# A hybrid layer stack over eight sequences: the loop over the sequences written out as straight code

## The reference

```python
def _layernorm(x): return (x - mean(x)) / sqrt(var(x) + 1e-5)

x = x + retention(_layernorm(x))      # 4 heads, chunks of tokens with a decaying state, gate, out projection
x = x + channel_mix(_layernorm(x))    # token shift, sigmoid(xr @ W_r) * (relu(xk @ W_k)**2 @ W_v)
x = x + attention(_layernorm(x))      # 16 heads of 16 features, softmax(q k / 4 + relative bias) v, out projection
x = x + channel_mix(_layernorm(x))    # the same weights as before
```

## Time and profile before

| | |
|---|---|
| median of three runs | 3388.71 us |
| lowest, highest | 3387.69, 3392.32 us |
| span of the profiled execution, first to last instruction | 3385.0 us |
| the profiled execution's own time | not given beside its span; the median is 3.7 us above the span |
| instructions recorded | 51303 |
| busy: PE, PEld | 3038.8 us (90%), 1389.2 us (41%) |
| busy: DVE, ACT, POOL | 2054.3 us (61%), 1713.4 us (51%), 1304.5 us (39%) |
| DMA | 108.66 MB, mean 32 GB/s |

### The profile page before, as it was taken

The page is one execution under the profiler, slowest core; times in us unless marked ns, Lnnn a source line. Parts: engine busy times, 40 slices in busy tenths (PEclk is TensorE's granted clock), DMA queues, the critical chain, the costliest instruction groups (busy, mean ns, idle before and its releaser), DMA issues.

```text
span 3385.0 us, 51303 instructions
## 1 busy us (share of the span) xinstructions
PE 3038.8 (90%) x14692; PEld 1389.2 (41%) x14692; DVE 2054.3 (61%) x3333; ACT 1713.4 (51%) x3668; POOL 1304.5 (39%) x1816
## 2 busy tenths in 40 slices
PE   6979999799997999879998799988999789997898
PEld 4623266223661236512365133652346523464224
DVE  4568645686456854478544785447854478544784
ACT  2427733377343763337633476334763347533575
POOL 2324533244332443424434244342443334433344
PEclk8979999799997999979999799997999979998899
DMA  5050000500004000140001300023000320003200
GB/s 147 13 112 1 2 14 13 112 2 1 14 24 101 1 1 14 42 83 1 1 14 51 75 1 1 14 58 68 2 7 8 68 58 1 8 8 74 51 1 13
DMA packets 71931, 108.66 MB, mean 32 GB/s; under 512 B 10896, under 2 KB 33472, under 8 KB 71488
## 3 DMA queue, kind: packets, MB, share of 16 engines
q1 hardware_dynamic: 71616, 104.91, 13.3%
HBM read 70.07 MB, written 36.72 MB: 32 GB/s over the span
## 4 chain that ended last, share of the span: by engine, by line
PE 64%; issue 8%; DVE 8%; DMA 7%; ACT 5%; POOL 4%; SPq 2%; ACTq 0%; DVEq 0%; POOLq 0%
PE psum L629 13%; PE psum L607 13%; PE psum L578 12%; PE psum L478 10%; PE psum L682 3%; DVE mx L1248 3%; DMA SQ<-mrow 2%; DMA SK<-parts 2%; ACT Z L999 2%; PE psum L663 2%; PE psum L723 2%; PE psum L497 2%; DMA parts<-Z 2%; POOL X L1338 2%; PE psum L709 2%
## 5 line engine op out<-in xcount | busy, mean ns | idle before, releaser
L1248 DVE TENSOR_REDUCE mx<-psum 128x1 f32<-128x1024 f32 x1024 | 1205.1, 1219 | 411.0 <-PE psum L578 411.0
L999 ACT ACTIVATE Z<-psum 128x512 f32<-128x512 f32 x2048 | 1103.5, 598 | 482.0 <-PE psum L607 479.7
L1426 POOL TENSOR_TENSOR Z<-Z,band_exp 128x256 f32<-128x256 f32 (+1 forms) x1152 | 713.0, 640 | 1040.2 <-ACT Z L999 1029.4
L578 PE MATMUL psum<-SK,SQ 96*128 96x512 bf16 x2048 | 626.2, 426 | 117.6 <-DMA SK<-parts 94.1
L607 PE MATMUL psum<-SQ,SK 128*128 128x512 bf16 x2048 | 647.7, 389 | 93.5 <-DMA SQ<-mrow 67.6
L629 PE MATMUL psum<-Z,Vx 128*17 128x512 f32 x4096 | 538.3, 599 | 4.2
L607 PEld LDWEIGHTS psum<-SQ,SK 128*128 128x128 bf16 x2048 | 165.4, 97 | 725.5 <-ACT Z L999 581.3
L478 PE MATMUL psum<-Wqkvg,Z 128*128 128x512 f32 x768 | 374.5, 614 | 25.0 <-ACT Z L906 22.5
L578 PEld LDWEIGHTS psum<-SK,SQ 96*128 96x128 bf16 x2048 | 189.7, 101 | 476.1 <-DVE mx L1248 179.3
L1368 POOL TENSOR_TENSOR Z<-Z 128x512 f32<-128x512 f32 x64 | 81.2, 1269 | 313.2 <-DVE Z L1177 313.2
L478 PEld LDWEIGHTS psum<-Wqkvg,Z 128*128 128x128 f32 x768 | 137.4, 191 | 153.5 <-issue 150.5
(11 more groups left out here) (124 smaller groups left out, 3363.6 us busy)
## 6 DMA issues: line engine op xcount, KB each, us to landing
parts<-Z SPq DMA_DIRECT2D x96, 256.0 KB
Xin<-L_attn_a_x SPq DMA_DIRECT2D x9, 1024.0 KB, 5.6
out<-X SPq DMA_DIRECT2D x16, 512.0 KB, 3.2
SQ<-parts SPq DMA_DIRECT2D x16, 384.0 KB, 6.4
SQ<-parts SPq DMA_DIRECT2D x24, 256.0 KB, 9.1
SK<-parts SPq DMA_DIRECT2D x16, 384.0 KB, 8.2
SK<-parts SPq DMA_DIRECT2D x24, 256.0 KB, 11.8
SQ<-parts SPq DMA_DIRECT2D x8, 768.0 KB, 8.8
```

The costliest lines, as they stand in the source:

```text
L578: mm = pe.matmul(bank[2 * (u % 2) + k], SQ[0:MAX_ROW, h, i * P:i * P + P], SK[0:MAX_ROW, h, 512 * k:512 * k + 512], start=True, stop=True)
L999: nc.scalar.activation(ring[:, n % RING, :], col_bank(s, c), ACT.Exp)\
L1248: nc.vector.tensor_reduce(mx[:, blk, col:col + 1], bank_pair[u % 2], AX_X, ALU.max)\
L1426: nc.gpsimd.tensor_tensor(ring[:, n % RING, a:z], ring[:, n % RING, a:z], band_exp[:, 4 * hg + c, at:at + z - a], ALU.mult)\
```

## The change

The five `Fori` loops become Python loops. `b` is then a number when the stream is written: the body stands eight times in each engine's stream, the loop's register, addition and branch are gone, and every value that a wait compares with is a constant. Work, order, tiles, semaphores and DMAs stay the same. The addresses of the loads of x and of the stores of the output, which depend on b, become constants too.

```diff
-            with sp.Fori(0, B) as b:
+            for b in range(B):
...
-            with pe.Fori(0, B) as b:
+            for b in range(B):
...
-            with act.Fori(0, B) as b:
+            for b in range(B):
...
-            with dve.Fori(0, B) as b:
+            for b in range(B):
...
-            with pool.Fori(0, B) as b:
+            for b in range(B):
```

## The result

The straight code is slower. Median of five runs 3399.81 us (3394.32 to 3403.2) against 3388.71 us of the kernel before; ratio 1.0027, 95% interval 1.0014 to 1.0039. The prediction was 3372.6 us and faster, its range 3361 to 3384: wrong in sign. The profiled execution took 3394.32 us, its span is 3392.3 us, 7.3 us more than the 3385.0 before.

What follows compares the result with a forecast made beforehand. TensorE held 64% of the chain, "issue" 8%; each sequence's end began with DVE's jump stall. Span 3385.0 - 13.6 (jumps) - 1.0 (register arithmetic) - 1.5 (clock) = 3368.9; with the median 3.7 over the span, 3372.6 us, range 3361 to 3384.

Steps and rivals of the forecast that it cites:

- The seven jumps: At seven sequence ends, straight code removes DVE's stall at the jump back and the whole gain arrives: minus 13.6 us.
- its 0.52 us: PE's idle time left before L478 at a sequence's end, the rest of its jump being hidden behind queued L527 matmuls.
- The register arithmetic: In all engines' streams, waits on registers become waits on constants, nearly all beside running instructions: minus 1.0 us.
- plus 1.2 us: Worst end of the register term: PE's double wait ahead of L478 costs 19 ns more on each of 64 token tiles.
- W: Follow-up theory, not in the prediction: attention's first exponential has its late wait on a separate instruction, 60 ns more, 27 us.
- the bodies were to keep their length to 0.5: Sign expected in the profile after: bodies between the sequence ends keep their length to 0.5 us.
- The clock: Short clock falls, as at the fifth sequence's start, become less likely with a shorter wait: minus 1.5 us, ends minus 5, plus 4.
- A: Rival, 9%: at the sequence ends L1171 waits for another result, only about 0.5 us returns at each of seven: 3385.1 us.
- B: Rival, 4%: at the sequence ends the jump is cheap, the 1.9 us have another cause; 2.1 us back at most: 3386.6.
- D: Rival, 5%: straight code arrives late through the instruction queues, about 3.5 us per late packet; ten late packets give 3408 us.
- a new "issue" of 2 us inside a sequence: Sign that the prediction is wrong: new idle time by "issue" of 2 us or more inside a sequence, pointing to D.
- C: Rival, 8%: register arithmetic in the engines' streams matters, its 10 us bound is used up: 3363.6 us.

## Why the prediction was wrong

**The seven jumps: right, mechanism and size.** Forecast 13.6 us, measured 13.3. L1029 follows L1308 directly, DVE's "issue" wait there is gone, and L1171 stands 0.24 us behind L1308, where under 0.4 was asked. L748 waits 1.20 us where 0.85 was forecast, mostly since PE came earlier: its last L473 ends 463.63 - 460.19 = 3.44 us behind L1308, where 3.70 was worked out; L748 itself starts 4.63 behind it, where 4.55 was. DVE's jump alone is worth 11.1 us in the part with the ends (367.4 to 356.3), PE's alone nothing (368.0), as the prediction had it: its 0.52 us count only once DVE's is gone.

**The register arithmetic: the step that failed.** The prediction wrote that an ALU_OP "that carries the first of two waits must, I assume, be replaced by an EVENT_SEMAPHORE that does", and counted 18 ns less on ACT. So it took the first of two waits to stay on the separate instruction. It did not: the first wait is now the instruction's own, and the second, at the exponential the late one, went to the EVENT_SEMAPHORE. The second error was to price the separate instruction by its own 17 or 51 ns, and not by the time from the semaphore's rise to the start of the work. That is 23 ns without one in the way and 83 with, and the row of durations can't show it. The third was to bound the cost by the share of the sequencers in the chain; this bounds what taking register instructions away can gain, not what a wait moved behind one can cost. The end of "plus 1.2 us" took a double wait of PE ahead of L478 for 19 ns dearer; it became 71 ns cheaper (113 to 42). Measured: +28.2 us in the attention, against 60 ns x 457 = 27 us by W. So the term that was put at minus 1.0 us, with plus 1.2 as its worst, has +28.2 us in the attention against it, and very likely the 12.8 us less in retention and first mix for it (see below). Per sequence that is 3.5 us more and 1.6 less, where the bodies were to keep their length to 0.5.

**Why 60 ns count in full.** In the chain of before, L999 has 2% and L607 and L629 26%, so I took the attention for PE's.

```profile
PE psum L629 13%; PE psum L607 13%; PE psum L578 12%; PE psum L478 10%; PE psum L682 3%; DVE mx L1248 3%; DMA SQ<-mrow 2%; DMA SK<-parts 2%; ACT Z L999 2%; PE psum L663 2%; PE psum L723 2%; PE psum L497 2%; DMA parts<-Z 2%; POOL X L1338 2%;
```

But PE and ACT are tied there: PE's fourth score matmul waits for the second exponential, which follows the first, which waits for the first matmul; and behind the fourth matmul PE has the weighing and then the next step's first matmul, in its own order. The list of waits said so, had I read it for this stage: ACT waited for L607 821 times, and PE's weight load of L607 for ACT 968 times. Each waits for the other in nearly every step, and that is a cycle, whatever engine the chain names.

**What the same term gained elsewhere.** Retention and first mix became 12.8 us shorter. The single engines give 4.1 (DVE), 1.7 (ACT) and 5.2 (PE), 11.0 in sum, but each is hardly more than what two profiles of one kernel differ by; the 12.8 us as a whole are not: the seven profiles with DVE, PE and POOL straight have 1199 to 1204 us there, the two with no straight code 1213.7 and 1216.5. The idle time of PE's weight loads of L478 fell from 153.5 to 143.6 us, before and after:

```profile
L478 PEld LDWEIGHTS psum<-Wqkvg,Z 128*128 128x128 f32 x768 | 137.4, 191 | 153.5 <-issue 150.5
```

```profile
L478 PEld LDWEIGHTS psum<-Wqkvg,Z 128*128 128x128 f32 x768 | 137.3, 190 | 143.6 <-issue 110.0 <-ACT Z L906 30.4
```

Most of what "issue" lost, 30.4 us, is the wait for z_T under its right name: it stood on an ALU_OP before and is L478's own now. The same turn, here for the better, is in the trace at other places of the retention, where the late wait is the one written first. From the semaphore's rise to the start it was 97 ns at ACT's L920, 102 at L927 and 113 at DVE's L1197, and is now 22 to 25. What each of them is worth was not tried by itself.

**The clock.** The kernel before had three short falls of 3.4 us each, at 1712.5 us, 2132.3 and 2927.7; after there is none. In the stretch of the first, from 8.6 us ahead of the fifth sequence's first L748, the granted clock is now 1.00:

```profile
1710.30:1730.30 20.00, 18.07 (x70) 10.34 (x69) 9.66 (x22) 7.00 (x22) 6.87 (x8) 1.00 0.08 27
```

The mean over the span went from 0.938 to 0.942. The direction is as forecast, the size of 1.5 us can't be told from the rest.

**The rivals.** A (something else takes the gain) and B (cheap jumps) fell: L748 waits 1.1 us less at the first end, and 13.3 us came back at the seven. D fell as a mechanism, though its sign came true: there are fewer instruction packets, and turning two waits round took the whole loss away. Its sign of being wrong, a new "issue" of 2 us inside a sequence, can mislead here: the view after has eight of up to 2.5 us ahead of PE's loads of L488, but the same waits stood there before, up to 2.6 us each, under DVE's L1131. The prediction, for its part, found no such "issue" before but at the jumps, and passed over one of 10.8 us on PE's loads of L607; it is a wait for a DMA and stands under that name after, with 10.9. The Trainium skill, "Runtime: NRT & Kernel Launch", section Instruction fetch mechanics, says that a taken branch to a target outside the two pages held needs a DMA fetch first; the trace agrees, as far as the 1.9 us of DVE's idle time vanish with the branch and the instruction packets become fewer. It adds that this is one reason why kernels prefer full unrolling; here that alone made the time 0.27% longer. C (the register arithmetic matters, 3363.6 us) had the gain nearly right, hidden by the turned wait: with the late wait first at seven places the time is 3366.5 and 3364.6 us. So the forecast's 3372.6 needed ACT's loop left as it was, and C's time the waits in the right order. No rival was the case that came: a second effect of the same edit, on the order of two waits, larger than the jumps and of the other sign.

## What to carry to other kernels

When waits change their form, from a register's value to a constant or back, look in the compiled program or the trace which wait of each pair the instruction itself carries, and see to it that it is the one that ends last. Here, with constants, that is the wait written first, with registers the one written last; turned the wrong way it costs 60 to 80 ns on ACT each time that the engine stands waiting. And before costing such an edit at nothing, look for pairs of engines that wait for each other in every step: in the cycle here ACT's 60 ns counted in full, though the chain names PE.

## What was not expected of the hardware

- From a semaphore's rise to the start of the instruction that waits for it, medians by the trace's semaphore events. ACT: 23 ns if the instruction carries the wait, 77 to 83 with an EVENT_SEMAPHORE ahead that carries it, 97 to 102 with an ALU_OP. DVE: 24, 92 to 101, 112 to 117. PE's weight load: 42, 105, 113. POOL: 68 if it carries the wait, and with an EVENT_SEMAPHORE ahead 133 (L1368, L1426), 155 (L1382) or, where that one holds two waits, 176 (L1322). The recorded durations of these instructions (17 to 51 ns) tell less than that.
- An ALU_OP that waits for nothing adds nothing to it on POOL: 68 ns ahead of L1368 and L1426.
- Straight code eight times as long brought fewer instruction packets: 118 and 92 on the two queues, where the loops had 143 and 172. With PE alone straight the first queue has 119 and the second stays at 172; with DVE or ACT alone the second has 150 or 141.
